# Graph attention kernel: GpSimd makes the first norm ahead of an older group's second, and one y in four

## The reference, cut to what matters

```python
# per graph, x and adj are [128, 128]
e      = leaky_relu((x * a_0) @ x.T, 0.2)
scores = where(adj == 1, e, NEG_INF)              # adj holds 0 and 1 only
x1     = layernorm(x + softmax(scores) @ x)       # first norm: this is y
h      = x1 @ W_loop.T
g      = h @ Wg_loop.T
vals   = (h + b_loop) * sigmoid(g + bg_loop)      # relation 1 is the only one present
out    = layernorm(x1 + relu(adj.T @ vals))       # second norm
```

## Time and profile before

| what | value |
|---|---|
| median of 3 runs | 185.68 us (184.71 to 185.92) |
| the profiled execution, its own time | 185.56 us |
| its span in the trace | 183.8 us |
| mean granted TensorE clock | 0.833 of full |
| busy: TensorE, VectorE, ScalarE, GpSimd | 127.4, 97.3, 86.8, 73.8 us |
| read from and written to HBM | 12.98 MB, 4.19 MB |

### The profile page before, as it was taken

How to read it: one execution, slowest core, us unless ns; L and a number is a source line. 1 busy time by engine, 2 the same in 40 slices (tenths; PEclk the granted TensorE clock), 3 DMA queues, 4 the chain that set the end, 5 groups by cost and what they waited for, 6 DMA issues and landing times. The chain is left out here.

```text
span 183.8 us, 2563 instructions
## 1 busy us (share of the span) xinstructions
PE 127.4 (69%) x684; PEld 111.8 (61%) x684; DVE 97.3 (53%) x390; ACT 86.8 (47%) x198; POOL 73.8 (40%) x125
## 2 busy tenths in 40 slices
PE   7567989386694939395876949494968868472920
PEld 7446688386674939385765839394857757352810
DVE  0123689193755739191937557382929476462440
ACT  3737788537362626546373636355473435110200
POOL 3000220907254351709072543618090725445273
PEclk9957999969697887969697988969696978876696
DMA  4999996511507070523401010101001010101012
GB/s 134 306 303 291 290 287 194 170 59 54 175 11 221 0 223 7 171 63 100 129 2 57 0 59 4 57 0 55 2 0 57 4 59 0 57 0 57 2 57 62
DMA packets 34769, 17.35 MB, mean 94 GB/s; under 512 B 1217, under 2 KB 34754, under 8 KB 34754
## 3 DMA queue, kind: packets, MB, share of 16 engines
q1 hardware_dynamic: 34608, 17.17, 34.0%
q10 hardware_dynamic: 146, 0.00, 0.0%
HBM read 12.98 MB, written 4.19 MB: 93 GB/s over the span
## 5 line engine op out<-in xcount | busy, mean ns | idle before, releaser
L677 DVE TENSOR_SCALAR y<-res,st,rs 128x128 f32<-128x128 f32 x64 | 17.9, 343 | 54.3 <-POOL rs L511 54.3
L772 PE MATMUL p_yt<-ident,y 128*128 128x128 f32 x64 | 17.7, 397 | 40.9 <-DVE y L677 40.9
L772 PEld LDWEIGHTS p_yt<-ident,y 128*128 128x128 f32 x64 | 10.4, 163 | 46.9 <-issue 43.1
L783 PE MATMUL p_hg<-w_both,y_t 128*128 128x256 f32 x128 | 37.7, 446 | 0.8 <-ACT y_t L606 0.8
L516 POOL TENSOR_SCALAR rs<-st 128x4 f32<-128x4 f32 x16 | 3.1, 194 | 81.2 <-DVE st L703 81.2
L783 PEld LDWEIGHTS p_hg<-w_both,y_t 128*128 128x128 f32 x128 | 29.8, 247 | 5.5 <-issue 0.9
L606 ACT ACTIVATE y_t<-p_yt 128x512 f32<-128x512 f32 x16 | 9.5, 596 | 49.2 <-PE p_yt L772 49.2
L794 PE MATMUL p_ag<-vals,mask 128*128 128x128 f32 x128 | 29.3, 404 | 0.3 <-DVE vals L686 0.3
L794 PEld LDWEIGHTS p_ag<-vals,mask 128*128 128x128 f32 x128 | 27.3, 313 | 0.8 <-DVE vals L686 0.5
L614 ACT ACTIVATE th<-p_hg 128x256 f32<-128x256 f32 x32 | 12.3, 384 | 28.2 <-PE p_hg L783 28.1
L645 DVE CUSTOM_DVE_ANT_0 nscore<-p_e,rel 128x128 f32<-128x128 f32 x64 | 14.7, 286 | 13.6 <-ACT rel L581 13.6
(11 more groups left out here) (52 smaller groups left out, 142.9 us busy)
## 6 DMA issues: line engine op xcount, KB each, us to landing
inputs<-x_t SPq DMA_DIRECT2D x16, 256.0 KB, 4.4
inputs<-adj SPq DMA_DIRECT2D x16, 256.0 KB, 4.7
inputs<-x SPq DMA_DIRECT2D x16, 256.0 KB, 4.8
out<-out_s SPq DMA_DIRECT2D x15, 256.0 KB, 2.3
out<-out_s SPq DMA_DIRECT2D x2, 128.0 KB, 1.8
w_rows<-w SPq DMA_DIRECT2D x1, 192.0 KB, 4.7
wg_s<-wg_t SPq DMA_DIRECT2D x1, 192.0 KB, 4.6
a_col<-a ACTq DMA_DIRECT2D x1, 0.5 KB, 3.0
```

The lines of the kernel that those rows point to most:

```text
L677: nc.vector.tensor_scalar(y[:, g % 4, i], res1[:, k, i], st1[:, k, i, 1:2], rs1[:, k, 1, i:i + 1], ALU.subtract, ALU.mult).then_inc(y_done, 1)
L772: last = nc.tensor.transpose(p_yt[:, i], y[:, g % 4, i], ident[:])
L783: last = nc.tensor.matmul(p_hg[:, i], y_t[:, g % 2, i], w_both[:], start=True, stop=True)
```

## The change

- GpSimd's order becomes `norm1` (1) and then `norm2` (3).
- `norm1` also makes y of the group's last graph (`tensor_scalar` with the mean and the reciprocal deviation as per-row scalars), behind a wait for its own power, and for the old readers of that y buffer; it signals with a new semaphore `y3_done`.
- `centre` on VectorE makes the other three, by `scalar_tensor_tensor` in place of `tensor_scalar`: the reciprocal deviation goes in as a second tensor, a 128x1 column broadcast to 128x128. All waits on `y_done` count three to a group, and the readers of y wait on `y3_done` too.
- SyncE's `load` is split: `load_scores` (x turned and adj, -5) and `load_values` (x, -4), so x comes a turn later in the queue; the weights come with x of group 0 and not of group 1.
- `mix_weights` moves on TensorE from ahead of `turn_probs` of group 0 to behind `attend` of group 0; `prepare_w` on VectorE from behind the scores of group 0 to behind those of group 1; ScalarE's two copies of the combined weights from ahead of `turned_probs` of group 0 to ahead of `turned_y` of group 0. The wait for the constants goes to `attend` of group 0.

```diff
-    "gpsimd": "norm2:3 norm1:1",
-    "sync": "load:-5 store:5",
+    "gpsimd": "norm1:1 norm2:3",
+    "sync": "load_scores:-5 load_values:-4 store:5",
...
+            def load_values(g):
                 sp.dma_start(x_s(g)[:, :, 0:P], x_v[g]).then_inc(x_loaded[g], 16)
-                if g == 1:
+                if g == 0:
...
                 if g >= 2:
-                    pool.wait_ge(y_done, G * (g - 1))
+                    pool.wait_ge(y_done, 3 * (g - 1))
                 nc.gpsimd.tensor_tensor(rs1[:, k, 1], rs1[:, k, 0], minus_half[:], ALU.pow).then_inc(rstd1_done, 1)
+                pool.wait_ge(rstd1_done, g + 1)
+                if g >= 4:
+                    pool.wait_ge(r2_done, g - 3)
+                    pool.wait_ge(ty_done, g - 3)
+                nc.gpsimd.tensor_scalar(y[:, g % 4, G - 1], res1[:, k, G - 1], st1[:, k, G - 1, 1:2],
+                                        rs1[:, k, 1, G - 1:G], ALU.subtract, ALU.mult).then_inc(y3_done, 1)
...
             def evac_ut(g):
-                if g == 0:
-                    act.wait_ge(w_pe, 1)
-                    ... (the two copies into w_both, now in evac_yt)
...
-                if g == 0:
+                if g == 1:
                     prepare_w()
...
-                for i in range(G):
-                    nc.vector.tensor_scalar(y[:, g % 4, i], res1[:, k, i], st1[:, k, i, 1:2], rs1[:, k, 1, i:i + 1],
-                                            ALU.subtract, ALU.mult).then_inc(y_done, 1)
+                for i in range(G - 1):
+                    nc.vector.scalar_tensor_tensor(out=y[:, g % 4, i], in0=res1[:, k, i], scalar=st1[:, k, i, 1:2],
+                                                   in1=rs1[:, k, 1, i:i + 1].broadcast_to([P, P]),
+                                                   op0=ALU.subtract, op1=ALU.mult).then_inc(y_done, 1)
...
             def transpose_u(g):
-                if g == 0:
-                    mix_weights()
-                else:
+                if g >= 1:
                     pe.wait_ge(ut_done, g)
...
             def attend(g):
...
+                if g == 0:
+                    mix_weights()
```

More of the change, by code:

```diff
@@ L153, in program @@
         y_done = sem("y_done")
+        y3_done = sem("y3_done")
         ty_done = sem("ty_done")
@@ L464, in _, with load_scores @@
         def _(sp):
-            def load(g):
+            def load_scores(g):
                 if g >= AHEAD + 1:
@@ L483, in store @@
                 sp.dma_start(out_v[g], out_s[:, k]).then_inc(stored[k], 16)
-            run("sync", {"load": load, "store": store})
+            run("sync", {"load_scores": load_scores, "load_values": load_values, "store": store})
             general_sync(sp)
@@ L592, in evac_ut @@
             def evac_ut(g):
-                if g == 0:
-                    act.wait_ge(w_pe, 1)
-                    nc.scalar.activation(w_both[:, 0:P], p_hg[:, 0, 0], ACT.Copy, scale=0.5).then_inc(w_ready, 1)
-                    nc.scalar.activation(w_both[:, P:2 * P], p_hg[:, 0, 1], ACT.Copy).then_inc(w_ready, 1)
                 act.wait_ge(tu_done, g + 1)
@@ L602, in evac_yt @@
             def evac_yt(g):
+                if g == 0:
+                    act.wait_ge(w_pe, 1)
+                    nc.scalar.activation(w_both[:, 0:P], p_hg[:, 0, 0], ACT.Copy, scale=0.5).then_inc(w_ready, 1)
+                    nc.scalar.activation(w_both[:, P:2 * P], p_hg[:, 0, 1], ACT.Copy).then_inc(w_ready, 1)
                 act.wait_ge(ty_done, g + 1)
@@ L655, in residual1 @@
                 if g >= 2:
-                    dve.wait_ge(y_done, G * (g - 1))
+                    dve.wait_ge(y_done, 3 * (g - 1))
+                    dve.wait_ge(y3_done, g - 1)
                 for i in range(G):
@@ L694, in residual2 @@
                     dve.wait_ge(cent_done, g - 1)
-                dve.wait_ge(y_done, G * (g + 1))
+                dve.wait_ge(y_done, 3 * (g + 1))
+                dve.wait_ge(y3_done, g + 1)
                 nc.vector.scalar_tensor_tensor(out=res2[:, g % 2], in0=p_ag[:], scalar=0.0, in1=y[:, g % 4],
@@ L740, in mix_weights @@
                 pe.wait_ge(b_loaded, 16)
-                pe.wait_ge(const_done, 7)
                 nc.tensor.matmul(p_hg[:, 0], mean_row[:], b_rows[:], start=True, stop=False, skip_group_check=True)
@@ L759, in attend @@
                 pe.wait_ge(x_loaded[g], 16)
+                if g == 0:
+                    pe.wait_ge(const_done, 7)
                 if g >= 1:
@@ L770, in transpose_y @@
                 for i in range(G):
-                    pe.wait_ge(y_done, G * g + i + 1)
+                    if i < G - 1:
+                        pe.wait_ge(y_done, 3 * g + i + 1)
+                    else:
+                        pe.wait_ge(y3_done, g + 1)
                     last = nc.tensor.transpose(p_yt[:, i], y[:, g % 4, i], ident[:])
```

## The result

The changed kernel takes 123.75 us (median of 4 runs, 123.48 to 124.58) against 185.45: a ratio of 0.668, 95% interval 0.664 to 0.672. The profiled execution has 123.48 us and a span of 121.6. The forecast was 125 us in a range of 119 to 147. (Ratios leave disturbed runs out and medians don't, so the two can differ a little.)

What follows compares the result with a forecast made beforehand. A chain of waits, GpSimd and VectorE in series at 10.13 us a turn, bounds the kernel. Start 27.6, twelve turns 73.2, last two 9.2, then the end: span 123.1, plus 1.76 around it, 125 us; range 119 to 147.

Steps and rivals of the forecast that it cites:

- The loop: GpSimd's first norm no longer waits behind an older group's second norm; VectorE's wait of 3.75 us a turn goes whole.
- What is late next: With that wait gone, ScalarE's loop is longest at 5.84 us, three engines within 0.16; 6.1 us a turn taken.
- y on GpSimd: The fourth graph's y in norm1 on GpSimd takes 0.35 us, bounds 0.28 and 1.0, and is hidden.
- Beside GpSimd: VectorE's y runs beside GpSimd's second norm, both on SBUF; costs 0.1 to 0.2 us, bounds nothing and 2.6.
- rival A: VectorE's y and GpSimd's second norm exclude each other on SBUF: 131.5, 143.5 or 151.5 us; chance 0.36.
- The copy at the start: Group 0's weights are made later, so group 2's products start at 18.25, not 19.35: gain 1.1 us.
- The sum: Whole run: group 1's y copy at 27.6, twelve turns, two last turns and the end give a 123.1 us span.
- the last two turns: At the end, turns without scores or products: 9.2 us for both, bounds 7.5 and 12.2.
- The clock: TensorE's granted clock, 0.84 between 100 and 110 us before, is 1.00 through the middle; already in the 5.84 us.
- B: TensorE's clock stays low because of its stands: 0.9 us more in each turn, 131.5 us; chance 0.08.
- C: GpSimd's y in norm1 becomes the bound and decides from 5.3 us; at 6.5 us, 188.5 us in all; chance 0.02.
- D: Another wait (store, y buffers) ties first and second norm, so the loop isn't opened: 184 us; chance 0.02.

Runs made afterwards that it cites:

- tensor_scalar_y: The changed kernel with VectorE's three y made by tensor_scalar again, the fourth still on GpSimd: 126.99 us, ratio 0.686.
- order_only: The kernel before with only GpSimd's order turned round, first norm ahead of second; four tensor_scalar y on VectorE, old start: 129.23 us, ratio 0.696.
- old_start: The changed kernel with loads, weights and their copies at the start as before: 125.92 us, ratio 0.677.
- order_and_power: The kernel before with GpSimd's order turned round and, in the second norm, the power ahead of the centring: 125.54 us, ratio 0.680.

## Why the prediction was right, and where its steps were off

**The loop.** Right, and shown both ways. The order alone gives 0.696 of the time, and everything but the order gives 0.979. The wait of 3.75 us a turn went nearly whole: 3.8 us of it are left in the whole run, in ten waits.

**What is late next.** I took turn 3 of the kernel before as the floor, 5.84 us with TensorE, VectorE and ScalarE within 0.16, and assumed 6.1. The turns are 5.75 and 5.89. TensorE is the first bound (its blocks were 5.74 apart in turn 3 already, and it is busy for all of 30 to 55 us), and the ScalarE loop that I read as 5.84 closes in 5.75. The second bound was not among those three: GpSimd.

**y on GpSimd.** The term was mis-sized. I took 0.35 us "near the select, whose shape it has", and said that it would be hidden up to 0.9; it takes 0.80 alone and 1.05 behind VectorE's y, and then sets the turn. My bound from above, 1.0, was where it ended. It cost 0.14 us a turn in the late form.

**Beside GpSimd.** Right in sum, wrong in the reading. I took 0.1 to 0.2 us, since no row showed a stretch. The exclusion of rival A is real: 0.44 us a turn with the order alone and 0.53 with four y of the new form. It doesn't show in the changed kernel because of the term just mis-sized. GpSimd's y of 0.80 us puts the centring, at 30.73, 1.19 us behind the end of GpSimd's power where I had it 0.65 behind, and by then VectorE's third y has started. Had it taken my 0.35, the centring would have come at 30.19, with VectorE's first y running since 30.10 and two to come, and one of those would probably have waited, as the third did in tensor_scalar_y. So, by this estimate, two errors cancelled, which is luck: VectorE was spared the exclusion because GpSimd's y was dearer than I thought. No run has a y of 0.35 us on GpSimd to show it. And the step that tied the exclusion to the new form's second SBUF tensor was wrong: order_only has the old form and pays as much. What it says of the Trainium skill's rule ("SBUF — State Buffer", section "Who interferes with whom"): the direction agrees, the later one waits; but the wait is shorter than the whole instruction, ending 0.20 us before the centring's end by the count above, and a power of 1.01 us on four columns holds nobody. The same section of the Trainium skill says that `tensor_scalar` can enter the two-port modes and can then contend with GpSimd, which the prediction had passed over; order_only's y of 0.8 us agrees, though no trace shows in which mode it ran.

**The copy at the start.** Right in direction, 1.1 us expected and 2.5 found in the profile (26.19 for 28.70). I had put the weights' matmuls at the low clock; in the profiled execution, with the group's products straight behind the transposes, the granted clock was 1.00 to 14 us, and the three matmuls took 1.6 us and not 2.4. The medians of old_start put the start at 2.2 us.

**The sum.** The last two copies of y that my sum named, groups 13 and 15:

```profile
96.14 0.60 ACT L615 ACTIVATE y_t<-p_yt 128x512 f32<-128x512 f32 x1 [1.07 <-PE p_yt L788]
...
108.08 0.60 ACT L615 ACTIVATE y_t<-p_yt 128x512 f32<-128x512 f32 x1 [2.98 <-PE p_yt L788]
```

| term | expected | found |
|---|---|---|
| copy of y of group 1 | 27.6 | 26.2 |
| twelve turns | 73.2 | 70.0 |
| the last two turns | 9.2 | 11.9 |
| from there to the end of the span | 13.1 | 13.5 |
| span | 123.1 | 121.6 |

The last two turns have no scores, but GpSimd's work in them is whole, so they take 5.89 and 6.05 us. That is the second step that missed GpSimd as a bound.

**The clock.** Right: 1.00 in the middle. Rivals B, C and D didn't happen; C's direction, GpSimd's y as the bound, did, at 1 us and not at 5.3.

## What to carry to other kernels

When two engines are in series inside one turn, look for work of an older group standing in front of work that a partner waits for: here the order of two steps in one queue took 30% off the time, nine tenths of all that the change brought. After that, look at when the instructions of VectorE and GpSimd that work on the same memory, SBUF, meet, not only at how long they are: moving the four-column power ahead of the 512-column centring in GpSimd's queue gave as much as moving work to it. An engine that is "hidden" with 0.1 us a turn to spare isn't; price it from both sides, in the last turns too.

## What the runs showed of the hardware

- GpSimd's `tensor_scalar` on 128x128 with two per-row scalars takes 0.797 us, where its select of the same shape took 0.283 and its `tensor_tensor` of four times the columns 1.05. Shape doesn't price an operation there.
- VectorE's y and GpSimd's centring exclude each other, whichever starts first, in both forms of y: the one with two SBUF tensors, and `tensor_scalar` with one. The later waited 0.44 to 0.9 us as VectorE, and 0.11 to 0.15 us as GpSimd; the 128x128 y in its way takes 0.34. A few hundredths of a us decide who waits (0.07 and 0.08 between the same two starts went opposite ways in order_and_power), so the same program can have two lengths of turn (5.84 and one of 6.7). GpSimd's y beside VectorE's is the milder case: 0.80 us when it is first, 1.05 when VectorE's is, which goes with the turns of 5.75 and 5.89.
- GpSimd's power on four columns takes as long as the centring, 1.01 us, and didn't hold y in either form.
- `scalar_tensor_tensor` with a broadcast column as its second tensor takes 0.347 us alone, and `tensor_scalar` with two scalars 0.342.
- One thing stays open: the 0.49 us gap of GpSimd at 50.1 us. It came once, ahead of the same group's output halves, in old_start and tensor_scalar_y too, and in no other run; no record names its releaser. The store two groups back, for which the halves also wait, isn't it: SyncE issued that at 39.97, and no store between 34 and 70 us took over 2.6 us to land. In tensor_scalar_y, where GpSimd stands 0.64 us in every turn, the gap changed no turn.
